# Weight chunks and product tiles turned by transposing DMAs, with the first stage's order rewritten

## What is computed

```python
# layer 0, attention part: rounded and clipped to 0..255, no softmax
x = x + fake_quant(layernorm(x)) @ fake_quant(ctx)          # per batch
# layer 0, feed-forward: block-scaled quantisation (blocks of 32 along the contraction)
h = fp6(layernorm(x))
g, u = h @ fp4(w_gate).T, h @ fp4(w_up).T                    # 1376 columns
x = x + fp6(silu(g) * u) @ fp4(w_down).T
# layer 1, attention: 32 query heads, 8 key and value heads of 128, rotary embedding
k, v = rope(ctx @ wk), ctx @ wv
x = x + softmax(rope(layernorm(x) @ wq) @ k.T + mask) @ v @ wo
# layer 1, feed-forward with ternary weights and scales
x = x + (silu(h @ gate_w.T * s0) * (h @ up_w.T * s1)) @ down_w.T * s2
```

## Time and profile before

| | us |
|---|---|
| median of 3 runs | 702.44 (700.72 to 703.03) |
| the profiled execution | 702.53 |
| its span | 700.7 |
| busy over the span: TensorE, VectorE, GpSimd, ScalarE | 668.3, 520.0, 463.3, 363.3 |
| DMA | 67.27 MB, mean 96 GB/s |

### The profile page before, as it was taken

How to read it: one execution, slowest core, us unless ns; L and a number is a source line. 1 busy time by engine, 2 the same in 40 slices (tenths; PEclk the granted TensorE clock), 3 DMA queues, 4 the chain that set the end, 5 groups by cost and what they waited for, 6 DMA issues and landing times.

```text
span 700.7 us, 11095 instructions
## 1 busy us (share of the span) xinstructions
PE 668.3 (95%) x3152; PEld 494.0 (70%) x3152; DVE 520.0 (74%) x1046; ACT 363.3 (52%) x686; POOL 463.3 (66%) x407
## 2 busy tenths in 40 slices
PE   6999998899899999999999999999999999799997
PEld 2444443444577788888888888888888877688885
DVE  4999798777668888888888888888888886721122
ACT  2697434533565665666666665665665663211110
POOL 0697426432479878778789788688698478066661
PEclk9999999999999999999999999999999999999999
DMA  9985422140323132141131221221223012013311
GB/s 340 343 293 183 134 87 80 36 155 6 127 71 119 30 106 76 30 134 45 55 110 45 82 83 45 90 75 46 89 75 135 17 31 66 25 46 101 113 56 61
DMA packets 39420, 67.27 MB, mean 96 GB/s; under 512 B 3680, under 2 KB 12000, under 8 KB 38368
## 3 DMA queue, kind: packets, MB, share of 16 engines
q1 hardware_dynamic: 39392, 66.93, 28.9%
HBM read 57.48 MB, written 9.44 MB: 95 GB/s over the span
## 4 chain that ended last, share of the span: by engine, by line
PE 71%; POOL 10%; DVE 8%; issue 7%; ACT 2%; DMA 1%; SPq 0%; POOLq 0%; DVEq 0%; ACTq 0%
PE ps L663 16%; PE ps L665 16%; PE ps L664 16%; PE ps L731 11%; PE ps L696 7%; POOL mx_raw L1104 3%; POOL mx_w L1110 3%; PE ps L584 2%; PE ps L520 1%; DMA X<-in_x 1%; PE ps L536 1%; POOL prob L1161 1%; PE ps L620 1%; DVE mx_amax L1339 1%; DVE stats L1260 1%
## 5 line engine op out<-in xcount | busy, mean ns | idle before, releaser
L1009 ACT ACTIVATE prob<-ps,nmax 128x512 f32<-128x512 f32 x128 | 88.3, 690 | 97.4 <-DVE nmax L1487 97.0
L1161 POOL TENSOR_SCALAR prob<-prob,rinv 128x512 f32<-128x512 f32 x128 | 89.4, 698 | 73.7 <-DVE rinv L1494 73.6
L731 PE MATMUL ps<-xt,wq_sb 128*128 128x512 f32 x384 | 103.2, 393 | 3.8 <-DVE q_cos L1502 2.1
L1020 ACT CAST pT<-ps 128x512 fp32r<-128x512 f32 x128 | 75.1, 587 | 52.8 <-PE ps L696 51.9
L1487 DVE CUSTOM_DVE_ANT_0 ps<-ps,mask_sb 128x512 f32<-128x512 f32 x128 | 87.9, 687 | 6.7 <-PE ps L665 6.3
L1508 DVE TENSOR_TENSOR pT<-ps,pT 128x512 fp32r<-128x512 f32 x128 | 86.3, 674 | 3.0 <-ACT pT L1020 2.0
L731 PEld LDWEIGHTS ps<-xt,wq_sb 128*128 128x128 f32 x384 | 71.6, 188 | 22.0 <-issue 4.6
L696 PE MATMUL ps<-idf,prob 128*128 128x128 f32 x512 | 76.7, 272 | 0.4 <-POOL prob L1161 0.3
L696 PEld LDWEIGHTS ps<-idf,prob 128*128 128x128 f32 x512 | 63.8, 141 | 17.3 <-POOL prob L1161 1.6
L520 PE MATMUL ps<-ctxT,wk_sb 128*128 128x512 f32 x128 | 60.5, 613 | 6.5 <-DMA ctxT<-in_ctx_cols 6.5
L1104 POOL TENSOR_TENSOR mx_raw<-mx_raw,mx_r 128x2048 f32<-128x2048 f32 (+1 forms) x9 | 30.2, 3354 | 53.7 <-DVE mx_r L1347 53.7
(11 more groups left out here) (177 smaller groups left out, 1587.9 us busy)
## 6 DMA issues: line engine op xcount, KB each, us to landing
mx_raw<-in_mxw SPq DMA_DIRECT2D x8, 1024.0 KB, 5.5
wq_raw<-in_wq SPq DMA_DIRECT2D x32, 256.0 KB, 3.2
wo_raw<-in_wo SPq DMA_DIRECT2D x32, 256.0 KB, 2.7
v_scr<-v_st SPq DMA_DIRECT2D x16, 256.0 KB, 2.5
kr<-k_scr SPq DMA_DIRECT2D x16, 256.0 KB, 2.9
vr<-v_scr SPq DMA_DIRECT2D x16, 256.0 KB, 3.4
k_scr<-k_st SPq DMA_DIRECT2D x14, 256.0 KB, 2.1
kr_swp<-k_scr SPq DMA_DIRECT2D x28, 128.0 KB, 3.3
```

Of the source, the lines that this page charges most:

```text
L731: last = mm(query_bank(H), wq_sb[:, par, l, k], xt[:, r, k], start=(n == 0), stop=(n == 11))
L1009: nc.scalar.activation(prob[:, j], bank(j % 2), ACT.Exp, bias=nmax[:, j:j + 1], scale=-1.0, accum_out=rsum[:, j:j + 1]).then_inc(exps, 1)
L1020: copy(pT[:, v % 2, 0, :, i * P:(i + 1) * P], bank(2 + i % 2).rearrange("p (k c) -> p k c", k=4)).then_inc(ph_ready, 1)
L1161: nc.gpsimd.tensor_scalar(prob[:, i], prob[:, i], rinv[:, i:i + 1], 1.0, ALU.mult, ALU.mult).then_inc(probs, 1)
```

## The change

1. TensorE no longer turns weight chunks. SP's queue issues one transposing DMA per chunk from `mx_w` to `WT` (`chunk_turn`), `scale_out(i)` waits for the turn of chunk i - 2, and `mx_turn` and `mx_keep` are gone.
2. The quantised rows `q1` are turned the first time by four transposing DMAs (`rows_turn`), behind the stores of step 1's first part.
3. The quantised products of row tiles 0 to 2 are turned by DMA (`inter_turn`); tile 3 still goes by TensorE and ScalarE.
4. The first loads are reordered (X first, context columns and value weights for the first units in four slices), the first four value units run slice by slice in four banks, key unit (0, 0) comes behind them, key unit (5, 1) moves into step 7.
5. GpSimd rotates the keys of head 0 behind `scale_out(0)` and behind `scale_out(1)` (before: ahead of the loop, and behind `scale_out(0)`), makes `mx_r` instead of VectorE, and scales in halves.
6. VectorE's row quantiser is two small passes shorter; a single-tile normalisation is two passes shorter.

```diff
-    ([("v", 0, 0), ("v", 1, 0), ("v", 2, 0), ("v", 3, 0)], [("k", 0, 1)]),
+    ([("v", 0, 0), ("v", 1, 0), ("v", 2, 0), ("v", 3, 0)], [("k", 0, 0), ("k", 0, 1)]),
...
-    ([("v", 7, 1), ("k", 5, 0)], []),
+    ([("v", 7, 1), ("k", 5, 0), ("k", 5, 1)], []),
 )
-LATE_KEYS = ((5, 1), (6, 0), (6, 1), (7, 0), (7, 1))
+LATE_KEYS = ((6, 0), (6, 1), (7, 0), (7, 1))
...
+            def slice_load(k):
+                sp.dma_start(ctxT[:, k, 0:CTX], ctx_cols[k * P:(k + 1) * P, 0:CTX]).then_inc(ctxT0_in[k], 16)
+                sp.dma_start(wv_sb[:, k, 0:512], wv[k * P:(k + 1) * P, 0:512]).then_inc(wv0_in[k], 16)
...
+            def chunk_turn(i):
+                n = 1 if i == NFULL else MXT
+                sp.wait_ge(mx_ready, 2 * NFULL + 1 if i == NFULL else 2 * i + 2)
+                sp.dma_start(WT[:, MXT * i:MXT * i + n].rearrange("p t (k r) -> p (t k) r", r=P), mx_w[:, i % 2, 0:n * D],
+                             transpose=True).then_inc(WT_in[i], 16)
+
+            def inter_turn(t):
+                sp.wait_ge(intq_ready, t + 1)
+                after(sp, down_sums, t - 1)
+                sp.dma_start(int_T[:, t % 2].rearrange("p (c r) -> p c r", r=P), int_q[:, t % 2], transpose=True).then_inc(int_in[t], 16)
+
+            def rows_turn():
+                sp.wait_ge(q1_ready, NT)
+                for t in range(NT):
+                    sp.dma_start(q1T[:, :, t * P:(t + 1) * P], q1[:, t], transpose=True).then_inc(q1T_in, 16)
...
-                stores(STEPS[i][0] + STEPS[i][1])
+                stores(STEPS[i][0])
+                if i == Q_AT:
+                    rows_turn()
+                chunk_turn(i - 1)
+                stores(STEPS[i][1])
             k_load(6)
 
-            sp.wait_ge(mx_turned, 2 * NFULL + 1)
+            for i in range(NFULL - 1, NCH):
+                chunk_turn(i)
+            for i in range(NFULL - 1, NCH):
+                sp.wait_ge(WT_in[i], 16)
...
             k_load(7)
+            for t in range(NT - 1):
+                inter_turn(t)
             wq_load(2, 0)
...
             def down(t):
-                pe.wait_ge(intT_ready, t + 1)
...
+                if t == NT - 1:
+                    pe.wait_ge(intT_ready, 1)
+                else:
+                    pe.wait_ge(int_in[t], 16)
...
             gate_up(0)
-            mx_turn(NFULL - 2, 0)
-            mx_turn(NFULL - 2, 1)
-            gate_up_slice(1, 0)
-            mx_turn(NFULL - 1, 0)
-            gate_up_slice(1, 1)
-            mx_turn(NFULL - 1, 1)
-            late_keys(0, range(0, 2))
-            gate_up_slice(1, 2)
-            mx_turn(NFULL, 0)
-            pe.wait_ge(mx_kept, 2 * NFULL + 1)
-            turn_inter(0)
+            gate_up(1)
             gate_up(2)
             down(0)
-            late_keys(0, range(2, 4))
-            turn_inter(1)
             gate_up(3)
             down(1)
...
             def scale_in(i):
+                m, p = width(i) // BLK, i % NRAW
+                pool.wait_ge(mx_expo, i + 1)
+                ts(mx_r[:, p, 0:m].bitcast(I32), mx_e[:, p, 0:m].bitcast(I32), -1.0, -(2.0 ** 24), ALU.mult, ALU.add).then_inc(mx_scale, 1)
                 pool.wait_ge(mx_scale, i + 1)
...
             def scale_out(i):
                 pool.wait_ge(mx_rounded, i + 1)
-                after(pool, mx_turned, 2 * (i - 1))
...
+                if i >= 2:
+                    pool.wait_ge(WT_in[i - 2], 16)
...
             scale_in(1)
-            key_rotate(0)
...
                 scale_out(i)
-                if i == 0:
-                    key_rotate(1)
+                if i < 2:
+                    key_rotate(i)
```

More of the change, by code:

```diff
@@ L216, in build @@
         ctx_in = [sem(f"ctx_in{i}") for i in range(2)]
-        ctxT_in = [sem(f"ctxT_in{i}") for i in range(2)]
-        wv_in = [sem(f"wv_in{i}") for i in range(2)]
+        ctxT0_in = [sem(f"ctxT0_in{k}") for k in range(KD)]
+        wv0_in = [sem(f"wv0_in{k}") for k in range(KD)]
+        ctxT1_in, wv1_in = sem("ctxT1_in"), sem("wv1_in")
         rk_in = sem("rk_in")
@@ L246, in build @@
         intq_ready, intq_turned, intT_ready = sem("intq_ready"), sem("intq_turned"), sem("intT_ready")
+        int_in = [sem(f"int_in{t}") for t in range(NT - 1)]
         down_sums, ffn0_done = sem("down_sums"), sem("ffn0_done")
@@ L287, in rotating @@
         def rotating(unit):
+            if unit == ("v", 0, 0):
+                return 0
             return ROTATE[place[unit] % len(ROTATE)]
-        def mx_bank(i, h):
-            return 2 if i in (NFULL - 2, NFULL - 1) and h == 1 else 0
         def keys_out(i, b):
@@ L483, in take, with turn_quantised @@
                 return rotating(unit)
-            def turn_quantised(turn):
+            def turn_quantised():
                 for h in range(2):
-                    n = take(("q", turn, h))
+                    n = take(("q", 1, h))
                     for k in range(2):
@@ L505, in attention0 @@
                     last.then_inc(l0_sums, 1)
[L507 to L511, removed]
-                    for k in range(KD):
-                        lo = t * D + k * P
-                        last = nc.tensor.transpose(bank16(n, HALF)[:, lo:lo + P],
-                                                   mx_w[:, i % 2, h * HALF + lo:h * HALF + lo + P], idb[:])
-                last.then_inc(mx_turned, 1)
             def key_part(i, b, n, parts):
@@ L522, in key_part, with first_values @@
                     last.then_inc(k_sums, 1)
+            def first_values():
+                units = STEPS[0][0]
+                for k in range(KD):
+                    pe.wait_ge(ctxT0_in[k], 16)
+                    pe.wait_ge(wv0_in[k], 16)
+                    for unit in units:
+                        i = unit[1]
+                        last = mm(bank(rotating(unit)), ctxT[:, k, i * P:(i + 1) * P], wv_sb[:, k, 0:512], start=(k == 0), stop=(k == KD - 1))
+                        if k == KD - 1:
+                            last.then_inc(v_sums, 1)
             def keys(i, b, n):
                 pe.wait_ge(wk_in[i % 2], 16 * (i // 2 + 1))
-                if i == 0:
-                    pe.wait_ge(ctxT_in[b], 16)
+                if (i, b) == (0, 1):
+                    pe.wait_ge(ctxT1_in, 16)
                 key_part(i, b, n, range(KD))
             def values(i, h, n):
-                if VALUES.index((i, h)) in (0, 4):
-                    pe.wait_ge(wv_in[h], 16)
-                if i == 4:
-                    pe.wait_ge(ctxT_in[1], 16)
+                if (i, h) == (0, 1):
+                    pe.wait_ge(wv1_in, 16)
                 for k in range(KD):
@@ L1276, in standardise @@
                 chain(ln, ts(r.bitcast(I32), var.bitcast(I32), -0.5, float(0x5F3759DF), ALU.mult, ALU.add))
-                for _ in range(3):
+                if hi - lo == 1:
+                    for three in (3.0, 3.0 * 2.0 ** 2, 3.0 * 2.0 ** 8):
+                        chain(ln, ts(step, r, var, r, ALU.mult, ALU.mult))
+                        chain(ln, stt(r, step, -three, r, ALU.add, ALU.mult))
+                    chain(ln, ts(r, r, -(2.0 ** -13), None, ALU.mult))
+                for _ in range(0 if hi - lo == 1 else 3):
                     chain(ln, stt(step, r, -0.5, r, ALU.mult, ALU.mult))
```

219 lines of the change are left out of this document (95 added, 124 removed).

## The result

The changed kernel takes 712.45 us (median of 4 runs, 711.78 to 713.38), the kernel before 701.74 us in the same session: a ratio of 1.015, 95% interval 1.0134 to 1.0166. So it is slower by some 10.7 us. I had forecast 705.0 us, slower by 2.6: the sign is right, the size is a quarter of what came. The profiled execution took 712.29 us, span 710.1.

What follows compares the result with a forecast made beforehand. Bound: TensorE and VectorE, both close to full in the first stage; after the change, chunk 5's load behind rotation 1 in SP's queue. First stage +4.3, second -1.7, so +2.6 us on 702.53: 705.0 us, range 693 to 718.

Steps and rivals of the forecast that it cites:

- T0: Start of feed-forward 0's first product on TensorE: 121.79 us before the change, forecast to move by +4.3 us.
- Rotation 1's end: GpSimd, first stage: the second key rotation ends at 52.2 us instead of 45.46, behind scale passes and rotation 0.
- 4.5 + R: SP's queue from rotation 1's end to chunk 5's load: 4.5 us as before, plus R = 6 for five transposing DMAs.
- The landing: Chunk 5's load lands 5.5 us after its issue at 62.7 us, so at 68.2 us.
- Peaks to key unit (3,0): VectorE from chunk 5's peaks to its read of layer 0's sums, which frees key unit (3,0)'s bank: 10.2 us.
- Key unit to T0: TensorE from key unit (3,0) to T0: 46.7 us instead of 47.65, plus 1.0 for the clock after its stand.
- the 0.9 us charged for the late first product turn: Second stage: the first product tile's turn, queued behind nine loads, comes 22 to 25 us after T0; cost 0.9 us.
- The 2.6 us gain: Second stage: without turns between gate and up products, the last clip ends 36.2 us after T0 instead of 38.8.
- (a): Rival, first stage: chunk 5's load doesn't bind; 698.8 us, or 691.3 with TensorE's sum alone as floor; chance 0.28.
- (b): Rival, SP's queue: each turn holds it until it lands, 17.2 us for five turns; 719 us; chance 0.14.
- (c): Rival, DMA: a turn's blocks run one behind another, 13.2 us for a chunk's sixteen; 755 us; chance 0.05.
- (d): Rival: cheap turns and the late load cancel, leaving the time within 2.1 us of before; chance 0.11.

Runs made afterwards that it cites:

- e1_load: On the changed kernel, SP issues chunk 5's load ahead of its waits for the two key rotations; 707.90 us, 1.0079 of the kernel before.
- f1_turn0: On e2_order, the DMA turn of row tile 0's quantised product is issued ahead of the later stages' loads; 695.08 us, 0.9895 of the kernel before.
- e2_order: On the changed kernel, SP issues chunk 5's load and chunk 0's turn before the rotation waits, row turns behind chunk 1's turn; 699.66 us, ratio 0.9957.
- f3_slices: On e2_order, TensorE runs two of row tile 3's three gate and up slices ahead of the first down product; 696.30 us, ratio 0.9909.
- g_copy: On the changed kernel, the nine chunk turns are plain DMA copies of the same bytes, without transposition; 710.22 us, 1.0106 of the kernel before.

## Why the forecast had the sign and not the size

**Right.** The mechanism of the first stage and the engines in its chain: the load behind rotation 1, VectorE idle for it, TensorE's stand for the bank that VectorE frees. Three of the signs that I had named are there: the load later than 58 us, over 5 us of idle for a DMA, TensorE idle before key unit (3,0). Two are not: T0 lies at 130.3 and not at 123 to 128 us, and the stretch behind it is 2.2 us longer and not 1.7 shorter. And one sign of being wrong is there: the turns of chunks 1 and 2 held SP's queue for 6.1 us each. They stood behind chunk 5's load, so they did not set its time. The first stage term by term:

- Rotation 1's end: 54.64 us against 52.2, +2.4. Scaling in chunk 2 began 1.0 us later than I had put it, the four passes in halves took 3.74 us instead of 3.64, GpSimd's new small pass 0.3, and rotation 1 took 5.16 instead of 4.36 us.
- 4.5 + R: 65.88 - 54.64 = 11.2 us against 10.5, +0.7. The turns held the queue for 7.6 us instead of 6, the middle of a wide bracket; the plain issues around them took 3.7 instead of 4.5.
- The landing: 6.4 against 5.5 us, +0.9. Over all eight chunks the median landing went from 5.5 to 7.6 us.
- Peaks to key unit (3,0): 9.7 against 10.2, -0.5. The second condition, which e1_load found, was in my chain nowhere, but the load was the later one. Another term was wrong and did not bind either: I had VectorE ready for chunk 5's peaks at 55.3 us, and it was ready at 59.5, as in the kernel before. X came 3.3 us earlier, but VectorE then waited 1.9 us for chunk 3's load and 1.9 for a lift, and two of its clips took 2.1 us longer.
- Key unit to T0: 48.3 against 46.7 plus 1.0 for the clock, +0.6; the clock took 1.8.

That makes T0 130.3 instead of 126.1: 4.2 us from small terms of mostly one sign. Rotation 1 and the landing are durations that I took from the trace of before; the rotation ran beside VectorE's clips (see the last section), and why the landing grew I did not test.

**Wrong.** The size is wrong by two equal parts: T0 moved by 8.5 us and not by 4.3, by the terms above, of which the end of rotation 1 is the largest; and the second stage has the wrong sign, +2.2 us instead of -1.7. There the step that failed is the 0.9 us charged for the late first product turn. The 2.6 us gain beside it is real: with the turn in time the stretch is 53.2 us and with TensorE's turns 52.4, where 55.28 - 2.6 gives 52.7. The last clip ended at T0 + 36.8 in f1_turn0, where I had 36.2, and at T0 + 41.0 in the changed kernel. And the times were nearly right: tile 0's product was ready at T0 + 13.6 (13.4 forecast), TensorE asked for it at T0 + 22.2 (21.5), it came at T0 + 25.6 (22 to 25). What I mis-sized is what the lateness costs: 57.7 - 53.2 = 4.5 us between e2_order and f1_turn0, 3.7 to f3_slices, not 0.9. I had priced the wait of the down product at the middle of its range and not followed what stands behind it: gate and up of tile 3 on TensorE, then VectorE, which paces the stage and waited twice, 1.9 and 1.8 us. The lower clock is part of it: the down product's ten passes took 4.47 us at a granted clock of 0.53 (155 to 161 us), against 2.32 at 1.00 in f1_turn0.

With these two, +4.2 and 57.48 - 53.6 = +3.9 us, the forecast's 705.1 becomes 713.2; the rest ran 1.3 us shorter than before and the time outside the span 0.4 longer, which gives the 712.3 measured.

**The rivals.** (a) fell for this kernel. With SP's queue reordered, the time is 699.7 us, where (a) had 698.8, but that is a coincidence: T0 is 116.5 and not 120.8, and the stage behind it 57.7 and not 52.7. (b) fell for the five turns ahead of the load: they hold the queue for 7.6 us and not 17.2, and chunk 0's turn lands 4.3 us after its issue and holds the queue for 2.1. It is nearer to the mark for a turn issued while transfers are under way: chunk 1's held the queue for 6.1 of its 8.2 us. (c) fell: a chunk's turn of sixteen blocks lands in a median of 4.3 us and at most 8.2, where (c) had 13.2. (d) fell: the time moved by 10.7 us. The landings also settle the two pages that I had weighed. By the Trainium skill (VectorE: DVE Perf Modes, The three transpose paths), sixteen blocks would be, as an estimate, 21 us; the trace does not bear that out. By the Trainium skill (Advanced Engine Details and Errata, X-Bar Transpose), a transposing DMA is about as fast as a plain one. The trace agrees only in part: the median landing is 4.3 us, against 3.0 in g_copy, and the queue is held for 2.06 us, against 0.47.

## What to carry to other kernels

When work moves from engines to DMA, price first the queue that issues it: list what stands behind each new entry and behind each wait ahead of it, and put the loads that others will need in front of any wait for a result. Here one order of the same instructions was 10.7 us slower and another 2.8 us faster than before, each against its own session's runs. A transfer that comes late costs not only its own wait but what that wait does to the engine that paces the stage, so follow the in-order queue behind the waiting instruction; and look for every condition that hangs on a late event, since removing the latest only uncovers the next.

## What the hardware showed that I had not expected

- A transposing DMA of 128x2048 bf16 between SBUF buffers held SP's queue for 1.7 us at least and for 6.1 us where transfers were already under way; a plain copy of the same bytes held it for 0.47 us. With the turns the core's packets under 512 B rose from 3,680 to 27,457; with the chunks' turns made plain copies they are 10,416.
- The turn of a 128x1408 product landed 3.5 us after its issue at best and took 9.6 us when issued behind nine loads.
- VectorE and GpSimd passes that overlapped took longer. In the changed kernel the context clip took 2.25 us and GpSimd's rotation pass beside it 2.25 us as well; the kernel before has the same rotation pass at 1.27 us, and in e1_load the same kind of clip took 1.22 us while GpSimd stood idle. Not every pair does this: VectorE's rounding passes from PSUM took 1.2 us beside GpSimd's scaling (54.6 to 59.5 us) as elsewhere. The changed kernel, then the pass of the kernel before, then e1_load:

```profile
49.59 2.25 DVE L1315 TENSOR_SCALAR ctx_f<-ctx_f 128x2048 f32<-128x2048 f32 x1
...
50.72 2.25 POOL L1120 TENSOR_TENSOR k_own<-k_own,ropeK 128x512 f32<-128x512 f32 x1
...
51.77 1.75 DVE L1366 TENSOR_SCALAR mx_q<-mx_q 128x2048 bf16<-128x2048 bf16 x1
```

```profile
42.78 1.27 POOL L1123 TENSOR_TENSOR k_own<-k_own,ropeK 128x512 f32<-128x512 f32 x1
```

```profile
61.62 1.22 DVE L1316 TENSOR_SCALAR ctx_f<-ctx_f 128x2048 f32<-128x2048 f32 x1
62.76 0.69 DVE L1367 TENSOR_SCALAR mx_q<-mx_q 128x2048 bf16<-128x2048 bf16 x1
```
